# Results of the first 22 tiles: stored plainly, with the nodes added to the output afterwards

## The reference

```python
h = jnp.maximum(_layernorm(x, axis=-1), 0.0)
# inside the layer, with h as its x:
h = jnp.einsum('ni,hif->hnf', x, W)
s1 = jnp.einsum('hnf,hf->hn', h, a1)
s2 = jnp.einsum('hnf,hf->hn', h, a2)
scores = jax.nn.leaky_relu(s1[:, :, None] + s2[:, None, :], negative_slope=0.2)
scores = jnp.where(adj[None] > 0, scores, NEG_BIG)
att = jax.nn.softmax(scores, axis=-1)
out = jnp.einsum('hnm,hmf->hnf', att, h)      # heads side by side: (N, 512)
# the result:
x = x + jax.nn.elu(out)
```

## Time and profile before

| | us |
|---|---|
| median of 3 runs | 772.41 (772.21 to 775.91) |
| the profiled execution | 777.28 |
| its span in the trace | 775.6 |
| PE, DVE, ACT, POOL busy in it | 575.2, 651.3, 477.7, 422.4 |
| bytes moved | 269.50 MB, 347 GB/s on average |
| stage one ends, first gather is issued | about 345, 351 |

### The profile page before, as it was taken

One profiled execution on the slowest core, in us unless ns is written; L12 is line 12 of the kernel. 1 busy time (PEld: TensorE's weight loads), 2 busy tenths in 40 slices (PEclk: granted clock), 3 DMA queues, 4 the chain that ended last, 5 costly groups with the idle time before them and its releaser, 6 DMA issues.

```text
span 775.6 us, 9118 instructions
## 1 busy us (share of the span) xinstructions
PE 575.2 (74%) x2184; PEld 408.2 (53%) x2184; DVE 651.3 (84%) x1966; ACT 477.7 (62%) x763; POOL 422.4 (54%) x805
## 2 busy tenths in 40 slices
PE   0479798898888788683767868685777659988672
PEld 0245454554444445353556657474656448776561
DVE  4659979899976776775879999999989988999983
ACT  0678977799898989925645666675655223334322
POOL 6634434353333332227766457657756876788850
PEclk9989899999888888875769888877788879999986
DMA  9999999999999999917999999999999887999994
GB/s 287 420 380 388 402 358 382 411 385 419 421 417 391 422 419 419 423 69 229 399 406 417 410 407 398 399 393 407 402 393 354 216 219 176 229 245 281 307 243 157
DMA packets 62395, 269.50 MB, mean 347 GB/s; under 512 B 12050, under 2 KB 12050, under 8 KB 49876
## 3 DMA queue, kind: packets, MB, share of 16 engines
q1 hardware_dynamic: 33520, 185.81, 59.5%
q0 software_dynamic: 25824, 77.31, 32.8%
q10 hardware_dynamic: 2996, 5.77, 2.0%
HBM read 243.49 MB, written 31.13 MB: 354 GB/s over the span
## 4 chain that ended last, share of the span: by engine, by line
DVE 21%; DMA 11%; POOL 10%; issue 8%; ACT 3%; PE 2%; DVEq 0%; ACTq 0%; POOLq 0%
DVE nodes L1156 9%; DMA nodes<-table,list_column 9%; POOL nodes L909 5%; POOL nodes L904 4%; DVE agg L1168 3%; DVE places L274 2%; ACT result L970 2%; DMA nodes<-table,column 2%; ACT result L972 2%; DVE best L263 1%; DVE to_row L1132 1%; DMA out_dram<-result 1%; DVE result L1176 1%; DVE owner L1097 0%; PE psC L1315 0%
## 5 line engine op out<-in xcount | busy, mean ns | idle before, releaser
L698 PE MATMUL psH<-sb_W,normedT 128*128 128x512 f32 x384 | 231.7, 695 | 0.0
L253 ACT ACTIVATE packed<-adj_rows,eight 128x3072 uint8<-128x3072 int32 x66 | 188.7, 2860 | 0.8
L904 POOL DMA_INDIRECT nodes<-table,column x138 | 137.4, 995 | 68.3 <-issue 39.9
L749 POOL TENSOR_TENSOR nodes<-nodes 128x520 f32<-128x520 f32 x47 | 60.9, 1296 | 154.2 <-ACT nodes L663 154.2
L1331 PE MATMUL psP<-nodes,ident 128*128 128x256 f32 x276 | 105.5, 471 | 50.4 <-issue 43.8
L909 POOL DMA_INDIRECT nodes<-table,list_column x109 | 110.1, 1010 | 57.7 <-issue 29.9
L1156 DVE TENSOR_TENSOR nodes<-nodes,psW 128x2048 f32<-128x2048 f32 (+4 forms) x66 | 138.7, 2141 | 0.0
L699 PEld LDWEIGHTS psS<-sb_Wa,normedT 128*128 128x128 f32 x384 | 80.5, 210 | 107.1 <-issue 107.1
L274 DVE FIND_INDEX8 places<-best,packed 128x8 uint32<-128x96 f32 (+6 forms) x240 | 109.9, 466 | 0.0
L263 DVE MAX8 best<-packed 128x8 f32<-128x96 f32 (+6 forms) x240 | 102.7, 459 | 6.4 <-ACT packed L253 6.4
L1332 PE MATMUL psP<-nodes,ident 128*128 128x264 f32 x276 | 102.1, 458 | 0.0
(11 more groups left out here) (182 smaller groups left out, 882.6 us busy)
## 6 DMA issues: line engine op xcount, KB each, us to landing
adj_rows<-in_adj_dram SPq DMA_DIRECT2D x66, 1536.0 KB, 10.2
nodes<-in_adj_dram SPq DMA_DIRECT2D x30, 1536.0 KB, 12.7
table<-nodes SPq DMA_DIRECT2D x48, 260.0 KB, 8.8
sb_x_rows<-in_x_dram SPq DMA_DIRECT2D x48, 256.0 KB, 9.1
out_dram<-in_x_dram SPq DMA_DIRECT2D x11, 512.0 KB, 11.3
result<-in_x_dram POOLq DMA_DIRECT2D x11, 512.0 KB, 7.9
out_dram<-result ACTq DMA_DIRECT2D x11, 512.0 KB, 4.6
out_dram<-result POOLq DMA_DIRECT2D x6, 512.0 KB, 6.5
```

What stands on the lines that cost most here:

```text
L253: nc.scalar.activation(words.bitcast(mybir.dt.uint8), sb["adj_rows"][buffer_of(i)][:], ACT.Square, bias=sb["eight"][:], scale=-17.0, accum ...
L698: nc.tensor.matmul(psH[:, t % 2], normedT[:, t % 2, kc], sb["W"][:, kc], start=(kc == 0), stop=(kc == KC - 1))
L904: nc.gpsimd.indirect_dma_start(out=nodes[:, node_at[u] + i * w.direct + j], out_offset=None, in_=table, in_offset=bass.IndirectOffsetOnAxi ...
```

## The change

The eleven copies of stage one go, and with them the accumulation of results onto them. The results of tiles 0 to 21 are stored plainly by ACT, in `store(u - 4)`, as soon as they are done; nothing has been added to them. The nodes of these tiles are added to the output afterwards: `add_to_stored(t)` on POOL reads 256 rows of x and accumulates them on the output, in HBM, as 128 pieces of 2 rows, and it waits first for the stores of these rows. It is called after the gathers (and after `add_x`) of units 21 to 31, once in each, for tiles 0, 2, ... 20. At the end SP waits for all eleven. `add_x` does nothing for groups 0 to 15 any more; `grow` always waits for `stored`.

```diff
--- before.py
+++ after.py
@@ -46,9 +46,9 @@
 XB = 6
 EARLY = 30
 HALF = N // 2
-COPY_TILES, COPY_ROWS = 2, 8
+PAIR_TILES, PAIR_ROWS = 2, 2
 HB = 3
-COPIED = tuple(range(0, 22, COPY_TILES))
+ADDED_LAST = 22
 KEPT = 4
 PACK = 4
 
@@ -214,16 +214,9 @@
     return sum(steps_of(s) for s in range(1, t))
 
 
-def copy_nodes(queue, sb, x, out, t):
-
-    rows = slice(t * P, (t + COPY_TILES) * P)
-    queue.dma_start(out[rows].rearrange("(p r) d -> p (r d)", r=COPY_ROWS),
-                    x[rows].rearrange("(p r) d -> p (r d)", r=COPY_ROWS)).then_inc(sb["copied"], 16)
-
-
-def lies_in_output(unit):
-
-    return all(t - t % COPY_TILES in COPIED for t in range(unit.tile, unit.tile + unit.tiles))
+def added_last(unit):
+
+    return unit.tile + unit.tiles <= ADDED_LAST
 
 
 def kept(unit):
@@ -549,8 +542,6 @@
                 for i in range(6, 2 * EARLY + 3):
                     if act_round[occupant(i)] == t:
                         load_adj(sp, sb, adj, i)
-                if t % 2 == 0 and 1 <= t // 2 <= len(COPIED):
-                    copy_nodes(sp, sb, x, out, COPIED[t // 2 - 1])
             sp.wait_ge(h_copied, TILES)
             sp.dma_start(table[(TILES - 1) * P + 1:N + 1], h_rows[:, (TILES - 1) % HB]).then_inc(stored[(TILES - 1) % HB], 16)
 
@@ -829,7 +820,9 @@
         node_sum_ready, mean_summed, mean_made, mean_stored = sem("node_sum_ready"), sem("mean_summed"), sem("mean_made"), sem("mean_stored")
         plan_step, centred, placed = sem("plan_step"), sem("centred"), sem("placed")
         gathered = [sem(f"gathered{u}") for u in range(AHEAD)]
-        x_added, stored, laid = ([sem(f"{n}{u}") for u in range(4)] for n in ("x_added", "out_stored", "out_added"))
+        x_added, stored = ([sem(f"{n}{u}") for u in range(4)] for n in ("x_added", "out_stored"))
+        laid = sem("nodes_laid")
+        PAIRS = ADDED_LAST // PAIR_TILES
         squared, owners, looked_up, facts_done = sem("squared"), sem("owners"), sem("looked_up"), sem("facts_done")
         sides_done = sem("sides_done")
         front_step, columns, added_s, leaky, shifted = sem("front_step"), sem("columns"), sem("added_s"), sem("leaky"), sem("shifted")
@@ -845,7 +838,11 @@
         ot = out.rearrange("(t p) d -> p t d", p=P)
         def out_written(g):
 
-            return 16 * sum(lies_in_output(v) == lies_in_output(GROUPED[g]) for v in GROUPED[g % 4:g + 1:4])
+            return 16 * len(GROUPED[g % 4:g + 1:4])
+
+        def nodes_added(g):
+
+            return 16 * sum(not added_last(v) for v in GROUPED[g % 4:g + 1:4])
 
         owned = [sum(w.n for w in UNITS[:u]) for u in range(U + 1)]
 
@@ -879,15 +876,19 @@
             def add_x(g):
 
                 w, o = GROUPED[g], g % 4
-                if kept(w):
+                if kept(w) or added_last(w):
                     return
                 pool.wait_ge(bent, g + 1)
-                if lies_in_output(w):
-                    if g == 0:
-                        pool.wait_ge(sb["copied"], 16 * len(COPIED))
-                    nc.gpsimd.dma_start(ot[:, w.tile:w.tile + w.tiles], result[:, o, 0:w.tiles], accum_op=ALU.add).then_inc(laid[o], 16)
-                else:
-                    nc.gpsimd.dma_start(result[:, o, 0:w.tiles], xt[:, w.tile:w.tile + w.tiles], accum_op=ALU.add).then_inc(x_added[o], 16)
+                nc.gpsimd.dma_start(result[:, o, 0:w.tiles], xt[:, w.tile:w.tile + w.tiles], accum_op=ALU.add).then_inc(x_added[o], 16)
+
+            def add_to_stored(t):
+
+                for g, w in enumerate(GROUPED):
+                    if t <= w.tile < t + PAIR_TILES:
+                        pool.wait_ge(stored[g % 4], out_written(g))
+                rows = slice(t * P, (t + PAIR_TILES) * P)
+                nc.gpsimd.dma_start(out[rows].rearrange("(p r) d -> p (r d)", r=PAIR_ROWS),
+                                    x[rows].rearrange("(p r) d -> p (r d)", r=PAIR_ROWS), accum_op=ALU.add, max_dma_last_dim=4096).then_inc(laid, 16)
             for u in range(HB):
                 pool.wait_ge(sb["table_stored"][u], 16 * (TILES // HB))
             pool.wait_ge(mean_stored, 16)
@@ -911,6 +912,8 @@
                                                  ).then_inc(gathered[k], 16)
                 if u >= 4 and UNITS[u - 4].last:
                     add_x(UNITS[u - 4].group)
+                if 0 <= u - (U - 1 - PAIRS) < PAIRS:
+                    add_to_stored(PAIR_TILES * (u - (U - 1 - PAIRS)))
             for u in range(U - 4, U):
                 add_x(UNITS[u].group)
 
@@ -927,8 +930,8 @@
                     sp.wait_ge(bent, g + 1)
                     sp.dma_start(ot[:, w.tile:w.tile + w.tiles], result[:, g % 4, 0:w.tiles]).then_inc(stored[g % 4], 16)
             for k in range(4):
-                sp.wait_ge(stored[k], 16 * sum(not lies_in_output(w) for w in GROUPED[k::4]))
-                sp.wait_ge(laid[k], 16 * sum(lies_in_output(w) for w in GROUPED[k::4]))
+                sp.wait_ge(stored[k], 16 * len(GROUPED[k::4]))
+            sp.wait_ge(laid, 16 * PAIRS)
 
         @block.scalar
         def _(act):
@@ -966,16 +969,19 @@
                 w, o = GROUPED[g], g % 4
                 act.wait_ge(agg_done, g + 1)
                 if g >= 4:
-                    act.wait_ge(laid[o] if lies_in_output(GROUPED[g - 4]) else stored[o], out_written(g - 4))
+                    act.wait_ge(stored[o], out_written(g - 4))
                 nc.scalar.activation(result[:, o, 0:w.tiles], agg[:, g % 2, 0:w.tiles], ACT.Relu, scale=-1.0).then_inc(below_done, 1)
                 act.wait_ge(below_done, g + 1)
                 nc.scalar.activation(result[:, o, 0:w.tiles], result[:, o, 0:w.tiles], ACT.Exp, scale=-1.0).then_inc(grown_done, 1)
             def store(u):
 
-                if u < 0 or not UNITS[u].last or lies_in_output(UNITS[u]) or kept(UNITS[u]):
+                if u < 0 or not UNITS[u].last or kept(UNITS[u]):
                     return
                 g, w = UNITS[u].group, UNITS[u]
-                act.wait_ge(x_added[g % 4], out_written(g))
+                if added_last(w):
+                    act.wait_ge(bent, g + 1)
+                else:
+                    act.wait_ge(x_added[g % 4], nodes_added(g))
                 act.dma_start(ot[:, w.tile:w.tile + w.tiles], result[:, g % 4, 0:w.tiles]).then_inc(stored[g % 4], 16)
             act.wait_ge(centred, 1)
             square(0)
@@ -1619,7 +1625,6 @@
             sb["early_listed"] = edges.enter_context(nc.semaphore("early_listed"))
             for name in ("keyed", "best_found", "searched", "checked", "cands_ready", "cut_step", "rose"):
                 sb[name] = edges.enter_context(nc.semaphore(name))
-            sb["copied"] = edges.enter_context(nc.semaphore("nodes_copied"))
             sb["adj_loaded"] = [edges.enter_context(nc.semaphore(f"adj_loaded{u}")) for u in range(6)]
             with ExitStack() as scan:
                 for name, shape, dtype in (("W", [P, KC, HF], F32), ("Wa", [P, KC, 2 * H], F32), ("x_rows", [P, XB, D], F32)):
```

## The result

The changed kernel takes 777.81 us, median of 20 runs (774.67 to 782.24). The kernel before took 775.64 us in the 20 runs beside them. The ratio is 1.0047, with a 95% interval of 1.0026 to 1.0067: slower by 3.6 us, and between 2.0 and 5.2 us (it is not the quotient of the two medians, which lie 2.2 us apart). The profiled execution of the changed kernel took 782.24 us, with a span of 780.5, 4.9 us longer than that of before.

What follows compares the result with a forecast made beforehand. ACT was taken to bound stage one, DVE the middle, and POOL's gathers, their lead used up, the tail's end. -0.5 - 2.5 - 0.2 + 10.8 + 2.0 = +9.6 on 772.4 gave 782.0 us, range 776 to 789.

Steps and rivals of the forecast that it cites:

- the band that was called not distinguishable from none: Whole kernel: about 0.5% around the old median, 768.5 to 776.3 us, taken as no change; chance 0.08.
- The fact on which it rested: Tail: POOL's lead over DVE is used up at the last unit; DVE already waited 0.49 and 0.51 us.
- POOL's term, 8 x 1.35 = 10.8 us: Tail, units 24 to 31: eight added accumulations each cost POOL 1.35 us before unit 32's gathers are issued.
- The engines' term, 2.0 us: Tail: DMA backlog from the new accumulations delays unit 32's last gather by 2.0 us, bounds 0 and 10.
- DMA engines bound the tail: Rival, tail: accumulations within HBM cost 3.6 us instead of 2.6, giving 788 to 792 us; chance 0.14.
- the condition that a gather is scored 3.3 us after its issue: Tail, unit 32: last gather awaited 3.3 us after issue, taken as evidence against the DMA engines as bound.
- The middle, 2.5 us: Units in the middle: with accumulating stores off POOL, DVE regains its 2.5 us of gather waits, bounds 0 and 2.5.
- Landing of ACT's stores, 8.8 us in the middle: Middle: ACT's plain stores land in 8.8 us, bounds 4.6 and 19.0, so `grow` loses nothing.
- ACT held in the middle: Rival, middle: 256 KB stores land in 14 us and hold ACT, +10, 792 us; chance 0.07.
- Stage one, 0.5 us with bounds 0 and 2.0: Stage one: dropping the eleven copies gives back 0.5 us of DVE's 2.0 us wait for late x rows.
- bound by bytes: Rival, stage one: bytes limit it, so dropping the copies returns 14 us, whole 768 us; chance 0.05.
- The rule that moving a transfer to another engine saves only its issue time: Middle: by this rule moving stores from POOL to ACT gains 0 instead of 2.5 us, forecast 784.5 us.

Runs made afterwards that it cites:

- light_adds: The changed kernel with each accumulation's 128 pieces cut from 4 KB to 512 bytes; 775.08 us, ratio 1.0014 to the kernel before.
- after_again: The changed kernel run once more, unchanged, for a second trace and ratio; 777.20 us, ratio 1.0062 to the kernel before.
- five_buffers: The changed kernel with five result buffers instead of four; 778.39 us, ratio 1.0066 to the kernel before.
- adds_at_end: The changed kernel with all eleven accumulations moved behind the last gathers; 796.35 us, ratio 1.0273 to the kernel before.
- four_and_buffers: The changed kernel with five 1 MB accumulations and one of 512 KB, plus five result buffers; 777.38 us, ratio 1.0082 to the kernel before.
- no_adds: The changed kernel without its eleven accumulations of x, so tiles 0 to 21 lack x; 770.60 us, ratio 0.9972 to the kernel before.
- copies_kept: The changed kernel without its accumulations, with the eleven stage-one copies put back; 769.67 us, ratio 0.9959 to the kernel before.
- no_copies: The kernel before without the eleven stage-one copies, nothing else changed; 770.38 us, ratio 0.9961 to the kernel before.
- adds_of_four: The changed kernel with five 1 MB accumulations and one of 512 KB, four result buffers; 790.10 us, ratio 1.0172 to the kernel before.

## Why the prediction was right where it was, and where not

*Direction and range.* Slower, and 777.8 us lies between 776 and 789. The range was built on a median of 772.4 us for the kernel before, which took 775.6 in the runs beside the change; 772.4 + 3.6 = 776.0 would have been its lower edge. That 777.8 lies clear of it is luck. But the forecast was +9.6 us, and measured are +3.6 (2.0 to 5.2) and +4.8 in the second comparison. The lower bound of the range was closer than the forecast. At +0.47% the change lies just inside the band that was called not distinguishable from none, to which only 0.08 had been given.

*The fact on which it rested* was right. DVE's lead over POOL was used up, and with the accumulations DVE waited 12.6 us for gathers in units 28 to 32; "some 12 us" was forecast, from unit 27 on. POOL went from 665 to 748 us without a pause.

*POOL's term, 8 x 1.35 = 10.8 us*, was mis-sized. POOL's starts behind units 24 and 32 lie 75.1 us apart before (670.24 and 745.32) and 83.2 after (665.24 and 748.42): 9.4 and 10.4 us a unit, so 1.0 us for each accumulation, 8.1 us in all, and light_adds shows 8.3. The step that failed took the price as the length of a round less ten gathers at 1.25 us. Some of those ten gathers took longer than 1.25, 0.3 us in all, and that was put on the accumulation; read directly, from the gather ahead of it to the gather behind it, it costs 1.0 us, alone or behind another transfer. The 1.01 of its own line in the earlier trace rows said the same. The forecast of 10.4 us a unit came true by luck, because the 9.05 us of the earlier trace rows was one of the short units; their mean was 9.4.

*The engines' term, 2.0 us.* The last gather of unit 32 was awaited 754.25 - 748.42 = 5.8 us after its issue, 2.5 more than before, and light_adds puts the bytes' part at 1.9 us. In after_again and five_buffers it was 4.9 and 5.0 us more, so the term was of the right kind, and 2.0 was too small against all three. The accumulation within HBM costs what was worked out: eleven of them and three x accumulations took 38 us of the engines in adds_at_end, 37 were set. At 788 to 792 us the rival "DMA engines bound the tail" falls. But four_and_buffers shows the engines as the next bound, and the condition that a gather is scored 3.3 us after its issue, which spoke against them, no longer held.

*The middle, 2.5 us*, was right in size. Units 14 to 17 took 48.8 us before (550.89 to 599.67) and 46.1 after (547.73 to 593.88), and 46.3 in no_adds and in copies_kept. One trace alone would not carry it: the same stretch took 47.4 us in no_copies, which still has the accumulating stores, and 47.5 in after_again, where unit 16 waited 1.1 us again. From unit 0 to unit 23 it is 303.2 and 303.5 us in the two traces with accumulating stores, and 299.1 to 305.9, median 300.8, in the twelve without. DVE also waited for gathers at units 0 to 2 (14.8 us before, 15.4 after), which the forecast left out; those waits did not move.

*Landing of ACT's stores, 8.8 us in the middle*: measured 9.4. No `grow` waited for one there; the rival "ACT held in the middle" falls. The same wait in the tail was overlooked: 37.6 us in seven waits, since the store lands in some 8 us and ACT reaches `grow` after 4.3. It was harmless only because the gathers were as late (five_buffers), and in adds_of_four it set the pace.

*Stage one, 0.5 us with bounds 0 and 2.0.* The two ratios that bear on it allow 0 to 3 us. Adding up the traces from the first scoring on, the changed kernel loses 7.4 us (780.5 - 363.26 against 775.6 - 365.72) and 8.7 in after_again; the timed runs lose 3.6 and 4.8. If the traces are typical, the missing 4 us lie ahead of the first scoring, where the means of the executions with and without copies differ by 362.8 - 358.1 = 4.7 us, part of which goes with the clock. Whether the copies cost 3 us, and by what wait, stays open: DVE's wait for x rows between 50 and 200 us was 2.0 us in both traces, so the term that the forecast named did not move. The rival "bound by bytes" falls in any case, since it asked for more than 10 us. With it falls, here, the reading by the Trainium skill's page "DMA: Bandwidth & Descriptors", section "Bandwidth": the changed kernel's stage one runs stretches at 419 GB/s. The same section gives the 358 GB/s as each core's part when both cores of a pair are streaming, and this kernel runs on one core.

*The rule that moving a transfer to another engine saves only its issue time* (the Trainium skill, page "DMA: Bandwidth & Descriptors", section "Issuing engines are not separate DMA queues") was read in the forecast as a gain of nothing in the middle. It does not say that: about 1 us of POOL's issue went from every round, and 2.5 us were gained where DVE waited for POOL. How much of them is issue time and how much the cheaper plain store, no run separates. light_adds shows the other side: where the issuing engine is the bound, issue time is most of the price.

## What to carry to other kernels

Before work is added to a queue, look up where its lead over its consumer ends: a lead that is used up at the last unit covers nothing, and 1 us a unit comes out whole. Read the price of an issue from the gather ahead of it to the gather behind it, and not from the length of a round. When two resources are nearly full, lowering one of them gives back little. An accumulation that only has to be done by the end belongs where its issuing engine pauses, and not in front of a transfer on the same queue that the last store waits for. A wait that carries many microseconds in the profile may be the second-latest of two; take it away before believing it (five_buffers), and expect it to bind once the loads grow (adds_of_four).

## What the runs showed of the hardware

- A direct transfer of 128 rows costs POOL 1.0 us between gathers, alone (653.02) or behind another (696.12), with 4 KB a row or 512 bytes (light_adds). One of 256 rows of 2 KB costs 1.35 us, an accumulation of 1 MB in HBM in 256 pieces 1.1 us. A second one starts 0.79 us after the first, and eleven in a row start 0.53 us apart (742.89 to 748.2).
- Within POOL's queue the order holds: an x accumulation behind eleven others was in only when they had drained, some 39 us later.
- Copies on SP's queue held back POOL's transfers more than accumulations in POOL's own queue did at the same share of the engines (1.06 and 1.07): the x accumulations landed in 15.1 us beside 11 MB of copies, in 8.9 beside the eleven accumulations of 512 KB.
- Ahead of the first scoring, executions with the same stage one differ by up to 10.8 us (354.0 to 364.8), more than the change is worth; the granted clock between 200 and 345 us was 0.90 and 0.83 in these two.
